# Causal mask moved from TensorE to a GpSimd select, projections in fp16 parts, and new engine orders

## The reference

```python
x = x + 0.5 * ffn(layernorm(x))     # 8 experts of 128x128, top 2 by a softmax router
x = x + attention(layernorm(x))     # 8 query heads, 2 key/value heads, head width 128, latent width 32
x = x + 0.5 * ffn(layernorm(x))
# in attention:
scores = einsum('bqhrd,bkhd->bhrqk', q, k) * scale
scores = where(tril(ones), scores, finfo.min)   # causal mask
probs  = softmax(scores)
```

## Time and profile before

| | us |
|---|---|
| median of 3 runs (lowest, highest) | 460.53 (459.79, 461.6) |
| the profiled execution, its time | 460.24 |
| the profiled execution, its span | 458.0 |
| busy PE, DVE, ACT, POOL (of the span) | 420.1 (92%), 376.5 (82%), 331.6 (72%), 315.4 (69%) |

### The profile page before, as it was taken

One profiled execution on the slowest core, in us unless ns is written; L12 is line 12 of the kernel. 1 busy time (PEld: TensorE's weight loads), 2 busy tenths in 40 slices (PEclk: granted clock), 3 DMA queues, 4 the chain that ended last, 5 costly groups with the idle time before them and its releaser, 6 DMA issues. The chain is left out here.

```text
span 458.0 us, 9994 instructions
## 1 busy us (share of the span) xinstructions
PE 420.1 (92%) x3233; PEld 203.1 (44%) x3233; DVE 376.5 (82%) x1199; ACT 331.6 (72%) x749; POOL 315.4 (69%) x413
## 2 busy tenths in 40 slices
PE   1886889999999999999999999999999999999961
PEld 0532434443644454455445554445435544533420
DVE  6796799999889978899889988998679899705674
ACT  3557447678897567998888865978978587898353
POOL 4396014269966817799499836399995439999966
PEclk9998899999999999999999999999999999999997
DMA  6202223002101010002001100031021000000001
GB/s 183 56 25 63 48 58 52 2 3 64 47 2 54 2 36 2 1 1 66 25 2 53 37 1 3 1 96 39 1 77 37 1 3 1 10 16 3 23 24 46
DMA packets 21123, 14.51 MB, mean 32 GB/s; under 512 B 2952, under 2 KB 20944, under 8 KB 21072
## 3 DMA queue, kind: packets, MB, share of 16 engines
q1 hardware_dynamic: 21072, 13.88, 11.6%
HBM read 3.78 MB, written 2.10 MB: 13 GB/s over the span
## 5 line engine op out<-in xcount | busy, mean ns | idle before, releaser
L769 ACT ACTIVATE prob<-bank,exp_scale 128x512 f32<-128x512 f32 x288 | 190.9, 690 | 49.4 <-PE bank L1296 35.9
L648 POOL TENSOR_TENSOR sums<-sums,prob 128x1024 f32<-128x1024 f32 x48 | 112.4, 2359 | 0.1
L1291 PE MATMUL bank<-q_stack,k_stack 98*128 98x512 f16 (+3 forms) x384 | 104.2, 327 | 1.9 <-DMA q_stack<-mT_lo 1.8
L1268 PE MATMUL bank<-k_stack,q_stack 96*128 96x512 f16 (+3 forms) x384 | 101.5, 329 | 2.2 <-DVE m_fin L1007 1.1
L734 ACT ACTIVATE scaled<-bank,gate 128x128 f32<-128x128 f32 x256 | 80.9, 373 | 25.5 <-POOL x L626 10.1
L1011 DVE TENSOR_REDUCE m_part<-bank 128x1 f32<-128x512 f32 x128 | 83.4, 674 | 4.7 <-PE bank L1268 4.3
L619 POOL TENSOR_TENSOR pair_sum<-dve_sum,scaled 128x256 f32<-128x256 f32 x64 | 46.5, 727 | 55.9 <-DVE dve_sum L991 51.0
L1007 DVE CUSTOM_DVE_ANT_0 masked<-bank,mask_qk 128x384 f32<-128x384 f32 (+1 forms) x128 | 76.0, 614 | 6.2 <-PE bank L1268 5.9
L1313 PE MATMUL bank<-prob,v_lat 128*32 128x512 f32 (+3 forms) x768 | 79.0, 494 | 0.2
L1291 PEld LDWEIGHTS bank<-q_stack,k_stack 98*128 98x128 f16 x384 | 36.3, 98 | 54.9 <-ACT prob L769 24.9
L1268 PEld LDWEIGHTS bank<-k_stack,q_stack 96*128 96x128 f16 x384 | 34.9, 98 | 45.0 <-issue 12.3
(11 more groups left out here) (145 smaller groups left out, 624.5 us busy)
## 6 DMA issues: line engine op xcount, KB each, us to landing
q_stack<-q_hi SPq DMA_DIRECT2D x32, 128.0 KB, 3.0
x<-in_L_attn_x SPq DMA_DIRECT2D x8, 256.0 KB, 3.3
q_stack<-q_lo SPq DMA_DIRECT2D x16, 128.0 KB, 3.1
out_x<-x SPq DMA_DIRECT2D x8, 256.0 KB, 2.4
k_stack<-k_hi SPq DMA_DIRECT2D x16, 64.0 KB, 2.7
we<-in_L_ffn_expert_weights SPq DMA_DIRECT2D x1, 512.0 KB, 4.2
x<-in_L_attn_wq SPq DMA_DIRECT2D x1, 512.0 KB, 6.5
x<-in_L_attn_wo SPq DMA_DIRECT2D x1, 512.0 KB, 7.8
```

The lines of the kernel that those rows point to most:

```text
L648: nc.gpsimd.tensor_tensor(into, first if j == 1 else into, new, ALU.add).then_inc(sum_step, 1)
L769: nc.scalar.activation(prob[:, n % NP, :], bank[ST + n % NST][:], ACT.Exp, scale=exp_scale[:, 0:1]).then_inc(p_ready, 1)
L1268: last = mm(into[:, n * w:(n + 1) * w], q_stack[0:MROW, c, g * NR + r, (i % TC) * P:(i % TC + 1) * P], k_stack[0:MROW, b % 2, g, k:k + w], ...
L1291: last = mm(into[:, at:at + CH - off], k_stack[:, b % 2, g, j * P:(j + 1) * P], q_stack[:, c, g * NR + r, off:CH], start=at == 0, stop=not ...
```

## The change

1. The mask product of the scores (L1296) and its constant `mask_kq` are gone. Instead GpSimd clears, in `prob` after the exponential, the elements above the diagonal with an `affine_select` (Z, 160 of them: 96 on 128x256 elements, 64 on 128x128). V of a diagonal group, and a sum that takes a diagonal tile, now wait for `cleared`, and no longer for the exponential alone.
2. Q, K and W are three products of fp16 parts each, and no longer one fp32 product. `aT` becomes `aT_hi` (ACT) and `aT_lo` (DVE, j, 8 steps), and three weights are split once (3 ACT steps, 3 DVE steps h, after a longer chain of unit steps).
3. The eight sums of the last quad (batch 3, c = 1, second head) are made by DVE and no longer by GpSimd, and counted by a semaphore of their own.
4. All orders are laid out anew.

```diff
+DIAGONAL = [n for n in range(NALL) for b, q, held in [score(n)] if on_diagonal(q, held[0][0])]
+CLEARED = {n: i + 1 for i, n in enumerate(DIAGONAL)}
+FIRST_LATE = 3
+def summed_late(b, q):
+    return b == NB - 1 and q >= FIRST_LATE
...
+            def clear_later(n):
+                held = score(n)[2]
+                step = max(1, held[-1][2] // P)
+                squares = prob[:, n % NP].rearrange("p (n q) -> p n q", q=P)[:, 0:held[-1][2] // P + 1:step]
+                pool.wait_ge(p_ready, n + 1)
+                nc.gpsimd.affine_select(out=squares, in_=squares, compare_op=ALU.is_ge, fill=0.0, base=0,
+                                        pattern=[[0, len(held)], [1, P]], channel_multiplier=-1).then_inc(cleared, 1)
...
+            last = b * NS + QSTART[q] + weights_at(q, j)[2 * pair + 1][0]
+            if on_diagonal(q, j):
+                engine.wait_ge(cleared, CLEARED[last])
+            else:
+                engine.wait_ge(p_ready, last + 1)
...
-                mm(into[:], aq[:, g * P:(g + 1) * P], x_part(n), start=True, stop=True).then_inc(q_done, 1)
+                mm(into[:], aq_hi[:, heads], hi, start=True, stop=False)
+                mm(into[:], aq_lo[:, heads], hi, start=False, stop=False)
+                mm(into[:], aq_hi[:, heads], lo, start=False, stop=True).then_inc(q_done, 1)
...
-                if diagonal:
-                    squares = into[:].rearrange("p (n q) -> p n q", q=P)[:, 0:held[-1][2] // P + 1:max(1, held[-1][2] // P), :]
-                    last = mm(squares, ident_b[:], mask_kq[:].unsqueeze(1).to_broadcast([P, len(held), P]),
-                              start=False, stop=True, skip_group_check=True)
...
-                pe.wait_ge(p_ready, group_end(b, q, j) + 1)
+                if on_diagonal(q, j):
+                    pe.wait_ge(cleared, CLEARED[group_end(b, q, j)])
+                else:
+                    pe.wait_ge(p_ready, group_end(b, q, j) + 1)
...
+                elif step == "A":
+                    add_weights(dve, V.tensor_tensor, *next(sums_to_make))
```

More of the change, by code:

```diff
@@ L157 @@
 SUMS = [(b, q, j, i) for b in range(NB) for q in range(NQ) for j in summed(q)[1:] for i in range(2)]
+FIRST_LATE = 3
+def summed_late(b, q):
+    return b == NB - 1 and q >= FIRST_LATE
+EARLY_SUMS, LATE_SUMS = ([s for s in SUMS if summed_late(*s[:2]) == late] for late in (False, True))
 MAXIMA = [(b, q) + m for b in range(NB) for q in range(NQ) for m in max_blocks(q)]
@@ L468, in route_bank, with wait_sums, add_weights @@
             return logits, turned, part, small
+        def wait_sums(engine, b, q, count):
+            if summed_late(b, q):
+                engine.wait_ge(late_step, count - len(EARLY_SUMS))
+            else:
+                engine.wait_ge(sum_step, count)
+        def add_weights(engine, add, b, q, j, pair):
+            Q, g = b * NQ + q, QUADS[q][1]
+            heads = slice(2 * pair, 2 * pair + 2)
+            new, first = (prob[:, at % NP:at % NP + 2, :] for at in
+                          (b * NS + QSTART[q] + weights_at(q, i)[2 * pair][0] for i in (j, 0)))
+            into = sums[:, g, heads, :]
+            last = b * NS + QSTART[q] + weights_at(q, j)[2 * pair + 1][0]
[3 more added lines that the diff above has]
+                engine.wait_ge(p_ready, last + 1)
+            if j == 1 and pair == 0:
+                need(engine, pv_done, (GROUP[b - 1, q, ORDER[q][-1]] + 1) if b else 0)
+            if j > 1:
+                wait_sums(engine, b, q, sum_done(b, q, j, pair) - 2)
+            add(into, first if j == 1 else into, new, ALU.add).then_inc(late_step if summed_late(b, q) else sum_step, 1)
         def home_of(use):
@@ L577, in _ @@
             select(mask_qk[:, CH - P:CH], 0, [[-1, P]], 1, ALU.is_ge, MASKED)
-            step(nc.gpsimd.memset(mask_kq[:], 0.0))
-            select(mask_kq[:], 0, [[1, P]], -1, ALU.is_ge, MASKED)
             step(nc.gpsimd.memset(mask_qk_b[:], 0.0))
@@ L659, in _ @@
                     normalise(next(outputs))
+                elif step == "Z":
+                    clear_later(next(to_clear))
                 elif step == "A":
-                    add_weights(*next(sums_to_make))
+                    add_weights(pool, nc.gpsimd.tensor_tensor, *next(sums_to_make))
         @block.scalar
@@ L685, in prepare_rest @@
                          bank[OB][:, g * P:(g + 1) * P].rearrange("p (r l) -> p l r", r=NR)).then_inc(prep_act, 1)
+                elif i > 4:
+                    act.wait_ge(peak_step, 7)
+                    hi, full = ((aq_hi, aq[:]), (down_k_hi, down_k[:]), (down_v_hi, down[:, NKV * DL:]))[i - 5]
+                    copy(hi[:], full, per_unit[:, i - 5:i - 4]).then_inc(high_split, 1)
                 else:
@@ L1061, in _ @@
             merges, den_steps = (Q for Q in range(NB * NQ) if QUADS[Q % NQ][0]), product(range(NB * NQ), range(3))
-            low_parts = [product([l], range(NN)) for l in (0, 2)]
+            low_parts, sums_to_make = [product([l], range(NN)) for l in range(3)], iter(LATE_SUMS)
             for step in DVE_ORDER:
```

244 lines of the change are left out of this document (130 added, 114 removed).

## The result

The changed kernel took 456.79 us (median) against 461.03 us for the kernel before on the same chip, a ratio of 0.9894 with a 95% interval of 0.9851 to 0.9936. It was run again beside the experiments: 456.61 us, ratio 0.9923 (0.9901 to 0.9944). The forecast was 447.7. Its time was 456.14 us, its span 454.4.

The account below looks back on a forecast made before the run. The prediction took TensorE to bound the middle and, with GpSimd, the last quads. Start 65, middle 307, last quads 39.5 and last tiles 34 make a 445.5 us span; 2.24 us beyond the span gives 447.7 us, range 438 to 460.

Parts of the forecast that it names:

- The bound of the kernel before: Middle, 67 to 395 us: TensorE, busy 326.6 of 328 us, sets the time; the middle costs its stream plus 9 us.
- Masks, projections, moved work: Middle: masks off TensorE save 12.8 us, fp16 projections 3.9, work moved by new orders the rest; 25.8 us less in all.
- I take 5 us of new gaps: Middle: TensorE's new idle time with DVE and GpSimd also near nine tenths, 5 us (0 to 16), giving 307 us.
- in 360 of 458 us a microsecond off PE is a microsecond off the time: Middle and last quads: TensorE's savings count fully as time, as long as DVE and GpSimd can follow.
- DVE and GpSimd in the middle: Middle: DVE busy 273 to 279 of about 307 us, GpSimd 278, its idle time under 35 us.
- The start: Up to the first score: 1 us off before the first maxima and 1 after, first score at 65 us (63.5 to 68).
- The last quads: After the last M: 7.6 us more on TensorE, so 31.5 us becomes 39.5 (38.5 to 43).
- POOL no longer full: Last quads: GpSimd stops being full as eight sums, 18.9 us, leave it for DVE at 1.2 us each.
- The end: Last feed-forward tiles: GpSimd has three tiles, 4.9 us, more work, partly in idle time; +2.5 us (0 to 5), 34 us.
- The select as a new wait: Rival, diagonal groups: selects queue behind 2.36 us sums on GpSimd and V on TensorE waits; 466 us, slower; chance 0.11.
- Another engine as the bound: Rival, middle: DVE or GpSimd locally over full, TensorE idles, only half the 26 us is gained; 458 us; chance 0.17.
- The port: Rival, after 395 us: DVE's eight sums and GpSimd's steps take turns at the shared memory port; +5, 453 us; chance 0.12.

Follow-up runs that it names:

- b_no_mask: The kernel before without its mask product and with nothing in its place, orders unchanged: 458.04 us, ratio 0.9948 to the kernel before.
- a_mask_on_pe: The kernel after without its selects and with the mask product back on TensorE, in the new orders: 466.11 us, ratio 1.0126 to the kernel before.
- a_warm: The kernel after with ten 512-column products of nothing ahead of the third quad's first maxima block in batch 0: 455.02 us, ratio 0.9853 to the kernel before.
- its two variants: The kernel after with the ten products, plus three key DMAs issued by ScalarE (455.73 us) or SP's DMAs of one stack put together (455.34 us).

## Why the prediction was wrong

**The bound of the kernel before: half right.** Shorter reductions and shorter exponentials left its middle within 0.7 us, so neither engine held it alone. But taking 12.8 us of steps off the same TensorE (`b_no_mask`) made it only 3.3 us shorter. TensorE was the fullest engine, and the others stood close behind it.

**Masks, projections, moved work, as TensorE's load: right in sum.** I forecast a middle of 302 us with the old gaps; TensorE was busy for 304.3 of it, and for 301.6 with the other engines lightened. Adding up the columns of all TensorE records between first score and last M, at 0.215 us for 512 columns (twice that for a record of an fp32 product, a quarter for products with 32 output rows), gives 303.9 us before and 277.8 after, 26.1 less where I had 25.8. The level is an estimate and lies below the 319 us of the prediction: what the middle has beyond it, 22.6 and 39.2 us, holds overheads and all gaps. I had the value projection wrong. At full clock, from its first record to the next instruction, it took 0.84 us in fp32 and 0.35 in fp16, so the seven W of the middle, taken as equal, save 0.49 us each. With the 4.1 us of 13 Q and 6 K that is about the 7.4 us by which fp32 projections lengthened the middle. The list was thus rather shorter than forecast, which makes the loss elsewhere larger.

**The step that failed: "I take 5 us of new gaps", and with it "in 360 of 458 us a microsecond off PE is a microsecond off the time".** The middle was 15 us over 302, at the top of the bound of 0 to 16 for the new gaps. I looked for them at the select, where there are next to none (317.2 without selects, 317.0 with). They came with the new orders: already with the masks on TensorE and no select, `a_mask_on_pe`, the middle was no shorter than before. The runs showed three sources in its place:

- Stops for DMAs into the stacks are 9.6 us of the middle, before 1.3. With all three engines light 6.0 us of them stay.
- 7.7 us go when reductions and exponentials are both shortened (4.5 and 0.6 singly).
- The half clock behind the stop at 62.5 us is worth 1 to 2 us, going by blocks 11 to 30 of `a_warm`.

These overlap and must not be added up. With short reductions the stop at 62.5 falls from 2.78 to 0.67 us, and blocks 11 to 30 take 19.4 us in place of 21.4, much as in `a_warm` (19.7).

I had written that of a moved step its DMAs count too, and then costed no DMA at all: the issues of 0.6 us and the landing of 2.7 to 3.1 us stood in the profile of the kernel before, and the shorter distance from Q and K to their M could have been counted in the strings. The one distance that I did take from them, 7.9 us between a score and its V, was that of the select.

**DVE and GpSimd in the middle.** DVE 280.6 us (forecast 273 to 279). GpSimd 261 in place of 278, its idle time 56 us, not under 35: selects were 0.31 and 0.41 us (forecast 0.29 and 0.45) and right, but the 144 of them in the middle took 50 us and not 56. I had also counted the rest too high there: by the trace 12 tiles left it and not 8, and it has two sums fewer, not one more.

**The start: too cautious.** First score at 59.5, forecast 65. From first maxima to first score DVE had 30 instructions (11.5 us) and before 62 (17.3); I had seen it full there, but took 1 us off where the stretch came out 6.3 us shorter. Projections are not the cause: with fp32 ones the first score was at 58.8.

**The last quads: 10.6 us longer, forecast 8.** GpSimd is at 92% there, so "POOL no longer full" was only just true. The eight sums on DVE were costed at 1.2 us; seven of them took 1.16 to 1.48, one 2.33 (it met a GpSimd step that had begun 0.7 us before it). What I left out of the sum and kept as a rival is the other side of it, the port that they share. The timeline of GpSimd and of DVE over two of them:

```profile
391.96 1.74 POOL L666 TENSOR_TENSOR pair_sum<-dve_sum,scaled 128x256 f32<-128x256 f32 x1 [0.35 <-DVE dve_sum L1048]
393.78 0.45 POOL L670 TENSOR_TENSOR pair_sum<-pair_sum 128x128 f32<-128x128 f32 x1
394.31 1.31 POOL L673 TENSOR_TENSOR x<-pair_sum,dve_sum 128x128 f32<-128x128 f32 x1
395.59 0.73 POOL L666 TENSOR_TENSOR pair_sum<-dve_sum,scaled 128x256 f32<-128x256 f32 x1
```

```profile
391.96 1.16 DVE L517 TENSOR_TENSOR sums<-prob 128x1024 f32<-128x1024 f32 x1
...
394.07 1.25 DVE L517 TENSOR_TENSOR sums<-sums,prob 128x1024 f32<-128x1024 f32 x1
```

The GpSimd step that meets a sum takes 1.74 us in place of 0.73, or 1.31 in place of 0.46. All eight sums have such a step beside them, longer by 0.8 to 1.0 us each, about 7 us of GpSimd in a stretch where it is at 92%. The Trainium skill, SBUF — State Buffer, section "Who interferes with whom", says that a DVE instruction with two SBUF inputs and a GpSimd instruction that reads SBUF exclude each other; this trace agrees. What of the 7 us is on the path is not shown. With all sums on a quarter of their columns, GpSimd's and DVE's eight, the last quads were 3.7 us shorter, with GpSimd busy 25 us of them and not 38; relieving both engines by less can hardly give more. Even so the move paid: the sums on GpSimd cost 12.4 us in this stretch.

**The end: right** (+2.7 for +2.5).

**The rivals.** The select as a new wait was wrong (4 us of waits, 1.6 to 2.0 us of time). Another engine as the bound was nearest in size (458), but with DVE and ScalarE by turns and the DMAs in the place of one full engine. The port was real, some 7 us of GpSimd's time; what it cost the kernel is not shown.

**What stays open.** How the 7.7 us that DVE and ScalarE hold divide between maxima blocks and the two score banks, as each alone gives 4.5 and 0.6 us of the middle; what of the 7.7 us of idle time that stay would go with the stops, as no run removed them all; and what a longer distance from projections to maxima would give, since TensorE's order itself was not laid out again.

The best version was `a_warm`, the kernel after with ten idle products in one stop: 455.0 us and 1.5% under the kernel before (1.2 to 1.8%); its two variants gave 1.3 and 1.4%.

## What to carry to other kernels

When most engines are near nine tenths, count a gain on the fullest one as a bound only, and test it before believing it: shorten each of the others in turn, and then together, since two that bind by turns show little singly. For each wait that a new order shortens the distance to, add up the whole chain behind it, DMA issues in one queue included; reordering that queue did not help here, as all its entries were needed by one reader. And when several parts change at once, undo one of them in the new orders: `a_mask_on_pe` was enough to see that the orders, and not the select, ate the gain.

## What the runs showed of the hardware

- A select on fp32 in SBUF took 0.31 us for 128x128 and 0.41 for 128x256, so by a straight line through the two the part that does not grow with the size is about 0.2 us.
- A sum of 128x1024 fp32 took 2.36 us on GpSimd and 1.16 at the shortest on DVE, where it held up the GpSimd step beside it by 0.8 to 1.0 us.
- A value projection of 4 x 64 columns took 0.84 us of TensorE as eight records of fp32 and 0.35 as twelve of fp16, both at full clock.
- From the last part of a projection to maxima that read its stack, over two splits, three to six DMA issues and their landing, took 6.9 to 8.9 us where TensorE waited for it.
- One stop of 2.78 us on TensorE was followed by a granted clock of 0.52 for 5 us; a stop of 1.80 us by 0.80.
